# Eleven chunks of NF4 weights: ten of them quantised in the layout that the matmul reads, with their scales spread over the partitions through memory

## What is computed

```python
x = layernorm(x + attn_ref(x, ...))      # gated block with six power terms, plus a feed forward of width 1248
x = layernorm(x + ffn_ref(x, w1, w2, w3))

def nf4_quant_dequant(w):                # blocks of 64 in a row of w
    flat = w.reshape(-1, 64)
    absmax = max(abs(flat), axis=1)
    normalized = flat / absmax
    idx = searchsorted(bounds, normalized)         # 15 bounds between 16 codes
    return (NF4_CODE[idx] * absmax).reshape(shape)

# ffn_ref: w1, w2 are 1376 x 512, w3 is 512 x 1376
h = silu(x @ dq1.T) * (x @ dq2.T)
out = h @ dq3.T
```

## Time and profile before

| | |
|---|---|
| time, median of 3 runs | 432.57 us (432.51 to 433.44) |
| the profiled execution | 432.66 us, span 430.9 us, mean granted clock 0.993 |
| PE busy | 418.3 us, 97% |
| DVE busy | 320.9 us, 74% |
| POOL busy | 272.3 us, 63% |
| ACT busy | 255.9 us, 59% |
| DMA moved | 26.50 MB, mean 62 GB/s |

### The profile page before, as it was taken

The page is one execution under the profiler, slowest core; times in us unless marked ns, Lnnn a source line. Parts: engine busy times, 40 slices in busy tenths (PEclk is TensorE's granted clock), DMA queues, the critical chain, the costliest instruction groups (busy, mean ns, idle before and its releaser), DMA issues.

```text
span 430.9 us, 5594 instructions
## 1 busy us (share of the span) xinstructions
PE 418.3 (97%) x1908; PEld 342.4 (79%) x1908; DVE 320.9 (74%) x393; ACT 255.9 (59%) x334; POOL 272.3 (63%) x216
## 2 busy tenths in 40 slices
PE   8999999999999899999999999999999999999992
PEld 6888888888778686888788888888888877888882
DVE  4549989979879954999859899899998885216025
...
PEclk9999999999999999999999999999999999999997
...
DMA packets 10875, 26.50 MB, mean 62 GB/s; under 512 B 1472, under 2 KB 1728, under 8 KB 10336
## 3 DMA queue, kind: packets, MB, share of 16 engines
...
...
## 4 chain that ended last, share of the span: by engine, by line
PE 79%; DVE 14%; issue 4%; DMA 1%; ACT 1%; SPq 0%; DVEq 0%
PE PS L1081 25%; PE PS L1083 25%; PE PS L1082 25%; DVE l_lo L826 3%; DVE PS L765 2%; PE PS L1196 2%; DVE h L811 1%; DMA h<-xT 1%; PE PS L1207 1%; DVE rcp L746 1%; DVE stats L840 1%; DVE amax L740 1%; DVE R L835 1%; DVE Q L772 1%; DVE R L811 0%
## 5 line engine op out<-in xcount | busy, mean ns | idle before, releaser
L1017 POOL TENSOR_SCALAR level<-side 128x1024 f32<-128x1024 int8 (+2 forms) x119 | 128.6, 1080 | 58.6 <-ACT side L530 35.4
L1081 PE MATMUL PS<-x_hi,w_hi 128*128 128x512 f32 (+1 forms) x352 | 138.4, 393 | 0.3 <-DVE x_lo L909 0.3
L1083 PE MATMUL PS<-x_hi,w_lo 128*128 128x512 f32 (+1 forms) x352 | 137.2, 390 | 0.0
L1082 PE MATMUL PS<-x_lo,w_hi 128*128 128x512 f32 (+1 forms) x352 | 137.1, 390 | 0.0
L765 DVE TENSOR_TENSOR PS<-PS,level 128x1024 f32<-128x1024 f32 (+2 forms) x102 | 121.6, 1193 | 5.2 <-POOL level L1017 1.7
L530 ACT ACTIVATE side<-Q 128x1024 int8<-128x1024 f32 (+1 forms) x77 | 77.6, 1048 | 15.3 <-DVE PS L761 9.6
L1045 POOL TENSOR_TENSOR l_lo<-h,l_hi 128x512 fp32r<-128x512 f32 (+1 forms) x42 | 56.0, 1340 | 45.0 <-ACT l_hi L530 44.6
L1081 PEld LDWEIGHTS PS<-x_hi,w_hi 128*128 128x128 f32 (+1 forms) x352 | 65.3, 185 | 14.9 <-issue 0.7
L1083 PEld LDWEIGHTS PS<-x_hi,w_lo 128*128 128x128 f32 (+1 forms) x352 | 65.2, 185 | 14.7
L1082 PEld LDWEIGHTS PS<-x_lo,w_hi 128*128 128x128 f32 (+1 forms) x352 | 65.3, 186 | 14.3
L1081 PE MATMUL PS<-x_hi,l_hi 128*128 128x512 f32 x144 | 57.1, 397 | 1.8 <-DVE l_lo L826 1.8
...
## 6 DMA issues: line engine op xcount, KB each, us to landing
Q<-w SPq DMA_DIRECT2D x20, 256.0 KB, 9.8
...
raw<-w_out SPq DMA_DIRECT2D x14, 256.0 KB, 2.6
...
out<-R SPq DMA_DIRECT2D x8, 256.0 KB, 2.0
raw<-w_fuse SPq DMA_DIRECT2D x7, 256.0 KB, 2.6
...
```

What stands on the lines that cost most here:

```text
L1017: g.tensor_scalar(level_of(s), side_of(s), LIMITS[k][1], LIMITS[k][0], ALU.min, ALU.max).then_inc(s_level, 1)
L1081: t_.matmul(dst, a_hi, b_hi, start=start, stop=False)
L1082: t_.matmul(dst, a_hi, b_lo, start=False, stop=False)
L1083: return t_.matmul(dst, a_lo, b_hi, start=False, stop=stop)
```

## The change

- Chunks 1 to 10 are "turned": SP loads each from an additional input `w12T`, in which the host has laid out w1 and w2 with the features on the partitions (`load_turned`), into `Q`. The same chunk in its natural layout is loaded too (`load_natural`), for the scales alone.
- The scales of a turned chunk are 16 numbers for each of up to 128 rows. SP stores `amax` and `rcp` to a scratch tensor in memory, transposed, in runs of one number (`to_memory`), and loads them back so that each row of blocks is spread over 64 partitions (`from_memory`: two DMAs for `rcp`, `rcp_back`, and two for `amax`, `amax_back`). Normalising on POOL and dequantising on DVE then multiply by full tiles. The steps between are as before.
- `transpose_nf4` is gone for the chunks 1 to 10 (`transpose_first` keeps chunk 0); `split_nf4` waits for the dequantising itself and reads `Q`, and so does `lo_nf4`.
- SP has a share of its own: `MOVES` in a fixed order, so many ahead of each raw weight's load. The spread `amax` takes the fifth raw slot: `RAW_SLOTS` = 4, `W_AHEAD` = 3. w3 is loaded after them, its first half once unit 10 is normalised.
- Scales of a turned chunk come 12 steps ahead of its first step, those of chunk 10 come 7 ahead.
- Eight subtractions of raw weights of stage 2 (`VECTOR_LOW`, jobs 13, 15, ... 27) move from POOL to DVE. In layer 2, every second product silu times up moves from DVE to POOL, for which ACT copies the up half out of PSUM (`up2`); TensorE's bank is then free at that copy.
- The last scale and shift of layer 1 on ACT comes behind the splits of token tiles 4 and 5. Slots of the left operand of the last two passes also wait for the dequantising of chunk 10, whose `amax` lies there.
- The shares of all engines are dealt anew. On DVE, before product 19 of layer 1, step (6,4) is reached in place of (6,1); in the terms that follow there are 2 adds in place of 3; chunk 10's scales stand ahead of `lo_nf4(1)`; behind that, 4 fewer steps are left. On POOL, the list of 31 and that of 32 steps in one place are spread out over the pairs of layer 2. On ACT, lines (10,0) and (10,1) stand ahead of the last scale and shift of layer 1.

```diff
@@ -115,8 +115,18 @@
 UNITS = C2 + 2 * W3_PARTS
+def turned(u):
+    return 0 < u < C2
+def block_rows(u):
+    return min(P, F2 - u * P) if u < C2 else P
 def unit_rows(u):
-    return min(P, F2 - u * P) if u < C2 else P
+    return P if turned(u) else block_rows(u)
 def w3_place(u):
@@ -141,11 +153,36 @@
 STEPS = [(u, k) for u in range(UNITS) for k in range(NB)]
-SCALES_AHEAD, NORMALISE_AHEAD = 5, 3
-def units_ahead(s, ahead):
-    return [u for u in range(UNITS) if max(0, NB * u - ahead) == s]
+TURNED_AHEAD, LAST_AHEAD, SCALES_AHEAD, NORMALISE_AHEAD = 12, 7, 5, 3
+def steps_ahead(u):
+    return SCALES_AHEAD if not turned(u) else TURNED_AHEAD if u < C2 - 1 else LAST_AHEAD
+def scales_due(s):
+    return [u for u in range(UNITS) if max(0, NB * u - steps_ahead(u)) == s]
+def normalise_due(s):
+    return [u for u in range(UNITS) if max(0, NB * u - NORMALISE_AHEAD) == s]
+MOVES = [(1, "scales"), (2, "natural")]
+for u_ in range(1, C2):
+    MOVES.append((u_, "rcp"))
+    if u_ + 1 < C2:
+        MOVES.append((u_ + 1, "turned"))
+        if u_ + 2 == C2:
+            MOVES.append((u_ + 1, "natural"))
+        MOVES.append((u_ + 1, "scales"))
+        if u_ + 2 < C2 - 1:
+            MOVES.append((u_ + 2, "natural"))
+    MOVES.append((u_, "amax"))
+MOVES += [(C2 - 1, "w3 first"), (C2 - 1, "w3 second")]
 def adds(s):
@@ -178,8 +215,10 @@
 AGAIN = [("out", f) for f in (0, 5, 1, 3, 4)]
 JOBS = ([("pre", 0)] + [("in", f) for f in range(C1)] + [(0, job) for job in FIRST_USE] + [(1, job) for job in AGAIN])
 JOB = {job: j for j, job in enumerate(JOBS)}
-RAW_SLOTS = 5
-W_AHEAD = 4
+VECTOR_LOW = [j for j in range(JOB[0, FIRST_USE[2]], JOB[0, FIRST_USE[-1]] + 1) if j%2==1]
+RAW_SLOTS = 4
+W_AHEAD = 3
@@ -197,28 +236,41 @@
 PAIRS2 = [(0, 0), (1, 0), (0, 1), (1, 1)] + [(f, half) for f in range(2, C2) for half in range(2)]
 PAIR2 = {pair: i for i, pair in enumerate(PAIRS2)}
+def on_pool(i):
+    return i % 2 == 1
+def multiplied(i, pool):
+    return sum(1 for x in range(i + 1) if on_pool(x) == pool)
 NORM_GROUPS = [range(0, 4), range(4, 6), range(6, 8)]
 W3_BANKS = 4
...
 SHARE = {
+    "sync": [
+        0, 2, 0, 2, 3, 4, 3, 2, 5, 3, 4, 3, 2, 3, 0, 0, 0, 0, 0, 0, 0, 0, 0, 2, 0, 0, 0, 2, 0, 3, 0, 7, 0],
     "scalar": [
...
@@ -384,13 +444,24 @@
         def wait_l_slot(eng, n):
             if n >= L_SLOTS:
                 wait_job_done(eng, n - L_SLOTS)
+            if n >= PASS_START[2]:
+                eng.wait_ge(s_dq, quantised(C2 - 1))
         def h_half(n):
             i, (kind, c) = SEQ[n]
             a, layer = i % 2, 1 if kind == "out" else 2
             view = h[0:job_rows(SEQ[n][1]), c * TOK + a * HALF:c * TOK + (a + 1) * HALF]
-            return view, (2 * c + a if layer == 1 else 2 * C1 + PAIR2[c, a]) + 1
+            return view, (s_h, 2 * c + a + 1) if layer == 1 else product_made(PAIR2[c, a])
+        def product_made(i):
+            return (s_h2, multiplied(i, True)) if on_pool(i) else (s_h, 2 * C1 + multiplied(i, False))
+        def bank_free(i):
+            return (s_up2, multiplied(i, True)) if on_pool(i) else product_made(i)
         def pair_of(layer, i):
@@ -406,6 +477,12 @@
         OUT_BANK = {1: (2, 3, 4, 5, 0, 1, 2, 3), 2: (0, 1, 2, 3, 6, 7, 4, 5)}
         NF4_BANK = 4
+        def nf4_chunk(f):
+            if f == 0:
+                return PS[:, NF4_BANK:NF4_BANK + 2, :].rearrange("p b n -> p (b n)")
+            return Q[:, f, 0:2 * DC * rows(f, F2)]
         def w3_bank(c):
             return 4 + c % W3_BANKS
@@ -422,9 +499,23 @@
         def w3_tile(q):
             return raw[:, q * PAIR:(q + 1) * PAIR]
+        def natural(u):
+            return Q[:, C2 - 1, :] if u < C2 - 1 else raw[:, 0:UW]
+        def rcp_wide(u):
+            return Q[:, C2 - 2, :] if u < C2 - 2 else Q[:, C2 - 1, :] if u < C2 - 1 else raw[:, UW:2 * UW]
+        def amax_wide(u):
+            if u == C2 - 1:
+                return l_hi[:, 0:2, :].bitcast(F32).rearrange("p s n -> p (s n)")
+            return raw[:, RAW_SLOTS * 1024:RAW_SLOTS * 1024 + UW]
         def unit_read(u):
             if u < C2:
...
@@ -479,9 +573,90 @@
                 sp.dma_start(w_raw(j)[0:p, 0:n], src).then_inc(s_raw[j % RAW_SLOTS], 16)
             def load_unit(u):
-                p = unit_rows(u)
-                sp.dma_start(Q[0:p, u, 0:D], w1[u * P:u * P + p, :]).then_inc(s_q[u], 16)
-                sp.dma_start(Q[0:p, u, D:2 * D], w2[u * P:u * P + p, :]).then_inc(s_q[u], 16)
+                p = block_rows(u)
+                to = natural(u) if turned(u) else Q[:, u, :]
+                sp.dma_start(to[0:p, 0:D], w1[u * P:u * P + p, :]).then_inc(s_q[u], 16)
+                sp.dma_start(to[0:p, D:2 * D], w2[u * P:u * P + p, :]).then_inc(s_q[u], 16)
+            def load_turned(u):
+                n = unit_width(u)
+                sp.dma_start(Q[:, u, 0:n], w12T[:, u * UW:u * UW + n]).then_inc(s_qT[u], 16)
+            def to_memory(u):
+                p = block_rows(u)
+                sp.wait_ge(s_prep, scaled(u))
+                if u >= 3:
+                    sp.wait_ge(s_at, 32 * (u - 2))
+                for k, t in enumerate((amax, rcp)):
+                    sp.dma_start(scr[u % 2, k, :, 0:p].rearrange("b f -> f b"),
+                                 t[0:p, u % t.shape[1], :], allow_slow_non_contiguous=True).then_inc(s_scr, 16)
+            def from_memory(u, k, to, done):
+                p = block_rows(u)
+                sp.wait_ge(s_scr, 32 * u)
+                blocks = scr[u % 2, k, :, 0:p].rearrange("(q r) f -> r q f", r=2)
+                for r in range(2):
+                    sp.dma_start(to[r * BLOCK:(r + 1) * BLOCK, 0:2 * DC * p].rearrange("p (q f) -> p q f", f=p),
+                                 blocks[r:r + 1].broadcast_to([BLOCK, 2 * DC, p])).then_inc(done, 16)
+            def load_w3(q):
+                sp.dma_start(w3_tile(q), w3[q * P:(q + 1) * P, :]).then_inc(s_w3[q], 16)
+            def rcp_back(u):
+                if u >= 2:
+                    sp.wait_ge(s_nrm, normalised(u - 1))
+                if u == C2 - 1:
+                    wait_split(sp, len(JOBS) - 1)
+                    wait_split(sp, VECTOR_LOW[-1])
+                from_memory(u, 1, rcp_wide(u), s_rc)
+            def amax_back(u):
+                if u >= 2:
+                    sp.wait_ge(s_dq, quantised(u - 1))
+                if u == C2 - 1:
+                    sp.wait_ge(s_tile, TT)
+                from_memory(u, 0, amax_wide(u), s_at)
+            def load_natural(u):
+                sp.wait_ge(s_prep, scaled(u - 1))
+                if u == C2 - 1:
+                    wait_split(sp, len(JOBS) - 1)
+                    wait_split(sp, VECTOR_LOW[-1])
+                load_unit(u)
+            def move(i):
+                u, what = MOVES[i]
+                if what == "scales":
+                    to_memory(u)
+                elif what == "rcp":
+                    rcp_back(u)
+                elif what == "natural":
+                    load_natural(u)
+                elif what == "amax":
+                    amax_back(u)
+                elif what == "turned":
+                    if u >= C2 - 2:
+                        sp.wait_ge(s_nrm, normalised(u - 1))
+                    load_turned(u)
+                elif what == "w3 first":
+                    sp.wait_ge(s_nrm, normalised(u))
+                    load_w3(0)
+                else:
+                    sp.wait_ge(s_dq, quantised(u - 1))
+                    load_w3(1)
+            turn, done = iter(SHARE["sync"]), [0]
+            def beside():
+                for _ in range(next(turn)):
+                    move(done[0])
+                    done[0] += 1
             def load_residual(a):
@@ -501,21 +676,19 @@
             load_job(1)
             load_unit(1)
             load_job(2)
-            load_unit(2)
+            load_turned(1)
             for j in range(3, RAW_SLOTS):
                 load_job(j)
             sp.dma_start(ident[:], ident_in).then_inc(s_ident, 16)
-            for u in range(3, C2):
-                load_unit(u)
             for j in range(RAW_SLOTS, len(JOBS)):
                 if j == JOB[1, AGAIN[0]]:
+                    beside()
                     load_residual(0)
+                beside()
                 load_job(j)
+            beside()
             load_residual(1)
-            wait_split(sp, len(JOBS) - 1)
-            for q in range(2):
-                sp.dma_start(w3_tile(q), w3[q * P:(q + 1) * P, :]).then_inc(s_w3[q], 16)
+            beside()
             for t in range(TT):
                 if t < TT - 1:
                     sp.wait_ge(s_norm, TT + t + 1)
@@ -593,6 +766,14 @@
                 dst = h_of(layer, i)
                 bank = pair_of(layer, i)[2]
                 nc.scalar.activation(dst, PS[0:dst.shape[0], bank, :], ACT.Silu).then_inc(s_silu, 1)
+                if layer == 2 and on_pool(i):
+                    k = multiplied(i, True) - 1
+                    if k == 0:
```

(53 more changed lines are left out.)

82 lines of the change are left out of this document (51 added, 31 removed), and 21 rows, old and new, of the table SHARE.

## The result

The changed kernel takes 531.68 us (median of 6 runs, 524.35 to 535.75), against 432.64 us for the kernel before in the same session: 1.223 times as long, 95% interval 1.216 to 1.230. The forecast was 426.2 us, faster.

A forecast was written before the change was run, and what follows sets the result against it. TensorE, busy 97% of 430.9 us, was taken to bound nearly everything. Terms -8.6 + 2.0 - 1.5 + 0.2 + 0 + 1.5 = -6.4 gave 426.3, stated as 426.2 us against the median; range 420.8 to 431.0.

The forecast's parts named there:

- the way through memory: Scales' stores and spread loads, chunk 10 the tight one: trip taken as 11.5 us, stall +1.5, bounds 0 to 22.
- the 10 allowed: Chunk 10: time in us its scales' trip may take before TensorE's last x transposes stall.
- rival C: Chunk 10's trip through memory stalls TensorE before the last x transposes; slower, 440 at X = 25; chance beyond old time 0.07.
- X: Time of chunk 10's scales' trip through memory, between scales and normalising: 7.5 to 32 us, taken as 11.5.
- The floor of about 7.5: Least time in us of chunk 10's trip: two landings of 2.6 and three pairs of issues.
- the 9 steps of cover: Chunks 1 to 9: 9 quantising steps, each with an add of 1.22 us at least, between scales and normalising.
- The gain: 80 transposes removed from TensorE, chunks 1 to 10, all in line on the engine that sets the end: 8.6 us.
- The terms' stretch: 128 to 152 us: VectorE's list changes while TensorE already waits, so lateness counts one to one: +2.0, bounds 0 to 5.
- The waits of 172 and 213 us: TensorE's waits of 1.0 on GpSimd and 0.5 on VectorE go: gain 1.5, bounds 0 to 1.5.
- The start: Scales of unit 1 now stand ahead of VectorE's first weight subtraction: +0.2, bounds 0 to 1.5.
- Layer 2: From 262 us: VectorE loses 8 products, but its w_lo subtraction has two SBUF inputs: 0, bounds 0 to 8.
- rival B: VectorE becomes the bound by shared SBUF reads: 437 at high bounds, halfway 430.5; chance 0.09 short of old time, 0.04 beyond.

The follow-up runs named there:

- the reciprocals first: Changed kernel with scales turned by VectorE, stored in 128-byte runs, and next chunk's reciprocals loaded ahead of this chunk's maxima on SyncE's queue: 435.52 us, ratio 1.006.

## Why the prediction was wrong

**Where it failed.** The step that failed is in the part on the way through memory: "A 4-byte run should be much nearer to the floor than a 2 KB packet; I take 11.5". It had both bounds in hand, 0 and 79 ns, and took the value near the lower end on a guess about size. By the time to landing, a run costs 78 ns. Chunk 10's trip, from the issue of its stores to its normalising, is 341.64 - 322.55 = 19.1 us against the 10 allowed, and TensorE idles the 7.7 us on `ACT R` shown above. By the prediction's own sum 9.1 were due. So the chunk that it did look at came out within its bounds: rival C, with X = 19.1 and a stall of 7.7, is what happened there. The floor of about 7.5 was right: with cheap stores and the reciprocals first, X is 236.56 - 228.91 = 7.7 us, and TensorE's wait for ScalarE is gone.

**The larger failure is the one of scope.** The prediction priced the stores once, as a latency, for the chunk with the least room, and waved the other nine through: "Chunks 1 to 9 have 9 quantising steps ... between scales and normalising". Price and place were not joined. Its own 79 ns would have said that a pair of stores holds the queue for 2 x 128 x 79 ns = 20 us, in every chunk. That queue also brings the raw weights, in a layer 1 whose chunks are normalised every 15.9 us. By that, ten pairs are some 200 us of queue. The second store of a pair that lands after 18.3 us, the load that waits 11.4 us behind one store, the 34 GB/s in 24 to 36 us, the 92 us of GpSimd's waits and the run of the old kernel with stores alone (34 us slower) bear this out. Of the 99 us, 83 go when the runs are made long.

**SyncE's order.** "SP's added waits hold back the raw loads queued behind", and these "are used 10 us or more later, and such a load lands in 2.6 us": that looked only at raw weights behind a wait. It didn't ask what the reciprocals stand behind: the maxima, whose tile comes free with a dequantising. That order is worth 14.7 us once the stores are cheap, and it makes the 9 steps of cover worthless: in the queue shown above the load leaves not when the scales are ready but 5.9 us ahead of its use (105.17 to 111.03). It is a wait that the change adds, and the sum had no term for it.

**The gain.** -8.6 was right in kind and size. In the kernel with the reciprocals first, 48 matmuls of layer 2 go from 280.02 to 290.90, 10.88 us, without a gap; the prediction said 10.9 for a chunk, where the earlier trace rows has 11.77.

**The terms' stretch**, +2.0 with bounds 0 to 5. In the earlier trace rows, 140 to 152 lacks 1.8 us of TensorE. With the reciprocals first, 132 to 144 lacks 3.1, and at the clock of 0.72 it does 28 matmuls where about 54 fit: 26 x 0.227 = 5.9 us of work in all, 4.1 more than before. It lies inside the bounds; 2.8 of it is the clock, for which the sum had no term, so that it stayed inside the bounds is partly luck.

**The waits of 172 and 213 us**, -1.5. Wrong in sign: with the reciprocals first, 168 to 180 lacks 2.0 us, where the earlier trace rows has 1.0 in the whole of 168 to 212, and the two later places named below lack 2.7 more. GpSimd is full in 168 to 180 (11.67 of 12). Each normalising went from 1.95 us in the earlier trace rows to 2.40. The prediction counted the normalising as 1.9, unchanged, though its second operand grew from 16 columns to 1024. That term is missing: 9 x 0.45 = 4 us on GpSimd. How much of the 2.0 it makes was not separated.

**The start**, +0.2 with bounds 0 to 1.5. Stage 2 of layer 1 begins at 128.32 us with the reciprocals first and at 127.26 before, and TensorE has no gap from 12 us to there in either. So the start costs 1.1, inside the bounds.

**Layer 2**, 0 with bounds 0 to 8. `w_lo` on VectorE averages 1.73 us instead of the 1.22 of the earlier trace rows, as rival B said, yet TensorE's gaps from 264 us on sum to under 1 us. The value taken was right, and the cover was there.

**The balance.** Sum up what TensorE lacks by stretches of 12 us from 132 us to the end of layer 2's products. Before it is 3.3 us. With the reciprocals first it is 8.7, of which 3.1 at 132 to 144, 2.0 at 168 to 180, 1.5 at 216 to 228 and 1.2 at 240 to 252, and the clock takes about 2.8 more: 8.2 us more than before. With the 1.1 of the start that is 9.3 against 8.6 gained, 0.7 in sum. The profiled executions of the two differ by 433.48 - 432.66 = 0.8. That profile is of the fastest of eight runs; the median is 2.0 us higher, and no trace here says where those lie.

**Rival B** as a whole has something to it, at another place: VectorE is held up in both layers, but in layer 2 TensorE hardly waits for it. Its price at the halfway point, 430.5 us, was nearer to the kernel with cheap stores and the right order (435.5) than the forecast.
